# Re-ordering six places of a two-layer transformer kernel, and folding the last two batches' gates into copies of the down-projection weights

## The reference, cut to what matters

```python
# layer 0, single-head attention and MLP, conditioned by film scale and shift
h = film(rmsnorm(x, norm1_w), cond, film1_w, film1_b)
x = x + softmax(q(h) @ k(h).T * 128**-0.5) @ v(h) @ proj_w + proj_b
h = film(rmsnorm(x, norm2_w), cond, film2_w, film2_b)
x = x + gelu(h @ mlp_w1 + mlp_b1) @ mlp_w2 + mlp_b2
# layer 1, 16 heads of 8 channels, padding mask, six vectors per batch from silu(cond)
mod = silu(cond) @ ada_w.T + ada_b
shift_msa, scale_msa, gate_msa, shift_mlp, scale_mlp, gate_mlp = split(mod, 6)
h = layernorm(x) * (1 + scale_msa) + shift_msa
x = x + gate_msa * (attention(h, mask) @ proj_w.T + proj_b)
h = layernorm(x) * (1 + scale_mlp) + shift_mlp
x = x + gate_mlp * (gelu(h @ fc1_w.T + fc1_b) @ fc2_w.T + fc2_b)
```

## Time and profile before

| what | value |
|---|---|
| time of the runs, median (lowest to highest) | 193.1 us (192.03 to 194.94), 3 runs |
| the profiled execution: its own time | 191.69 us |
| its span, first to last instruction | 189.9 us |
| mean granted TensorE clock in the span | 0.990 |
| busy: TensorE, VectorE, ScalarE, GpSimd | 173.1, 121.1, 107.7, 98.7 us |

### The profile page before, as it was taken

One profiled execution on the slowest core, in us unless ns is written; L12 is line 12 of the kernel. 1 busy time (PEld: TensorE's weight loads), 2 busy tenths in 40 slices (PEclk: granted clock), 3 DMA queues, 4 the chain that ended last, 5 costly groups with the idle time before them and its releaser, 6 DMA issues.

```text
span 189.9 us, 5687 instructions
## 1 busy us (share of the span) xinstructions
PE 173.1 (91%) x2250; PEld 134.2 (71%) x2250; DVE 121.1 (64%) x357; ACT 107.7 (57%) x272; POOL 98.7 (52%) x166
## 2 busy tenths in 40 slices
PE   6876989999699999889999999996997999999993
PEld 6744877587276698677678777875886765678592
DVE  0693598978005069768756876699489665596233
ACT  2336957862683751577577756673774785723500
POOL 5599949899900805994004333675145086691000
PEclk9999999999999999999999999998899999999999
DMA  5999999412650300300110000100000000001103
GB/s 126 345 430 423 433 412 431 177 43 52 217 224 0 114 0 3 116 5 5 57 60 3 7 35 31 57 5 2 5 7 7 2 3 0 5 0 55 59 0 110
DMA packets 5190, 19.31 MB, mean 102 GB/s; under 512 B 556, under 2 KB 1148, under 8 KB 3836
## 3 DMA queue, kind: packets, MB, share of 16 engines
q1 hardware_dynamic: 4844, 18.27, 25.0%
q10 hardware_dynamic: 320, 0.68, 1.2%
HBM read 7.24 MB, written 1.09 MB: 44 GB/s over the span
## 4 chain that ended last, share of the span: by engine, by line
PE 44%; issue 20%; POOL 19%; DVE 9%; DMA 3%; ACT 3%; POOLq 0%; DVEq 0%; ACTq 0%
PE ps L337 8%; PE ps L328 7%; PE ps L315 6%; PE ps L307 6%; POOL xb L1196 3%; POOL gtmp L1194 3%; POOL xc L1189 3%; PE ps L265 3%; POOL rstd L1115 3%; PE ps L366 2%; DMA xs<-x 2%; POOL xs L1203 2%; POOL gated L1200 2%; ACT hT L661 2%; DVE bn L844 2%
## 5 line engine op out<-in xcount | busy, mean ns | idle before, releaser
L1002 DVE TENSOR_REDUCE nm<-ps 128x4 f32<-128x512 f32 x64 | 42.0, 683 | 18.3 <-PE ps L366 17.9
L739 ACT ACTIVATE shared<-ps 128x512 f32<-128x512 f32 x64 | 34.5, 596 | 22.0 <-PE ps L366 21.9
L366 PE MATMUL ps<-k_pad,q_pad 32*128 32x128 f32 x512 | 35.4, 284 | 5.0 <-DVE nm L1002 4.7
L366 PEld LDWEIGHTS ps<-k_pad,q_pad 32*128 32x128 f32 x512 | 30.1, 188 | 13.2 <-issue 6.5
L366 PE MATMUL ps<-q_pad,k_pad 32*128 32x128 f32 x512 | 35.5, 285 | 0.1
L366 PEld LDWEIGHTS ps<-q_pad,k_pad 32*128 32x128 f32 x512 | 29.7, 188 | 0.5 <-DMA q_pad<-nmT 0.5
L1115 POOL TENSOR_TENSOR rstd<-var_eps,half 128x4 f32<-128x4 f32 x16 | 16.4, 1023 | 24.5 <-DVE var_eps L858 17.0
L1200 POOL TENSOR_TENSOR gated<-attn,gate 128x128 f32<-128x128 f32 x16 | 7.3, 459 | 40.8 <-ACT attn L758 40.7
L432 PE MATMUL ps<-shared,vx 128*32 128x128 f32 x512 | 17.9, 282 | 0.5 <-ACT attn L758 0.3
L785 ACT ACTIVATE hid<-ps,W 128x512 f32<-128x512 f32 x16 | 10.9, 689 | 9.7 <-PE ps L328 9.7
L307 PE MATMUL ps<-hT,W 128*128 128x512 f32 x32 | 14.6, 598 | 1.7 <-ACT hT L661 1.7
(11 more groups left out here) (127 smaller groups left out, 321.9 us busy)
## 6 DMA issues: line engine op xcount, KB each, us to landing
q_pad<-hid SPq DMA_DIRECT2D x1, 4096.0 KB, 21.7
k_pad<-hid SPq DMA_DIRECT2D x1, 4096.0 KB, 30.6
gate<-gates SPq DMA_DIRECT2D x1, 2048.0 KB, 7.2
xs<-x SPq DMA_DIRECT2D x4, 256.0 KB, 6.4
gate<-mask SPq DMA_DIRECT2D x1, 1024.0 KB, 11.9
q_pad<-apT SPq DMA_DIRECT2D x4, 256.0 KB, 2.4
k_pad<-apT SPq DMA_DIRECT2D x4, 256.0 KB, 2.4
W<-weights SPq DMA_DIRECT2D x1, 768.0 KB, 9.9
```

Source lines behind the costliest of these rows:

```text
L366: return mm(bank(to)[:, t], held[some, t, b], moved[some, t, b], start=True, stop=True, skip_group_check=True)
L739: a(pT[b % 2][:, r], bank(of), ACT.Exp, scale=HD ** -0.5).then_inc(s["c_exp"], 1)
L1002: v.tensor_reduce(nm[b % 2][:, 4 * r:4 * r + 4], bank(of), AX.X, ALU.max, negate=True).then_inc(s["c_max"], 1)
```

## The change

Nothing of what is computed changes. In the order of the lists:

1. VectorE's silu(cond) goes from behind `a_residual(0)` to ahead of the first `hT` (its wait for `a_T`).
2. ScalarE does `a_kv(0)` ahead of `affine("a_", 1, ...)`.
3. `b_up(1)` and `b_gelus(1)` are cut in two halves, and the transposition and `affine` of group 2 stand between the halves.
4. V of the second group is made in two halves of two batches in bank 7, in `between(2)` and `between(3)` (`second_value`), and copied by ScalarE in two halves (`second_v`); `project_v(1)`, `front_v(1)` and the wait of `between(3)` for them are gone. `behind(3)` waits for the second half's copy.
5. `d_norm(0)` and `d_norm(1)` leave VectorE. GpSimd does them (`first_norm`), at its b = 11 and b = 15; its `d_bias(0)` moves from b = 11 to b = 12.
6. GpSimd makes, at b = 13 and 14, a copy of the `fc2` weights times the gate of batch 14 and of batch 15 (into `hc`, free by then). `d_last` uses them for the last two batches, each into a place of its own (banks 6 and 2), so that VectorE has one addition per batch in place of a multiplication and an addition for the pair. Each of the two is sent by itself: six transfers out instead of five.

```diff
-            for n, (b, size) in enumerate(((0, G), (G, G), (2 * G, G), (3 * G, 2), (3 * G + 2, 2))):
+            for n, (b, size) in enumerate(((0, G), (G, G), (2 * G, G), (3 * G, 2), (B - 2, 1), (B - 1, 1))):
...
+            def d_last(j, o_bank):
+                pe.wait_ge(s["d_w2"], j - 1)
+                for f in range(FC):
+                    ins = mm(bank(o_bank)[:, j], hid[1][:, f, j], hc[j % 2][:, f], start=(f == 0), stop=(f == FC - 1),
+                             skip_group_check=True)
+                ins.then_inc(s["d_M2"], 1)
...
+            def second_value(half):
+                if half:
+                    pe.wait_ge(s["c_vh"], 1)
+                for j in (2 * half, 2 * half + 1):
+                    mm(ps[:, 7, N * (j % 2):N * (j % 2) + N], hc[1][:, j], w("v1"), start=True, stop=True,
+                       skip_group_check=True)
...
-                if g % G < 3 and g // G + 1 < B // G:
+                if g % G < 3 and g != 2 and g // G + 1 < B // G:
                     pe.wait_ge(s[("c_q", "c_k", "c_v")[g % G]], g // G + 2)
...
                     pe.wait_ge(s["c_h"], b + LEAD)
+                    if b in (2, 3):
+                        second_value(b - 2)
                     turn_x(b + LEAD)
...
-                    pe.wait_ge(s["c_v"], (b - 3) // G + 1)
+                    pe.wait_ge(s["c_v"], max(2, (b - 3) // G + 1))
...
-                if g < B // G and b % G < 3:
+                if g < B // G and b % G < 3 and b != 2:
...
-            b_up(1)
+            b_up(1, range(2))
             m_norm("b_", 2, 4)
+            b_up(1, range(2, FC))
...
-            d_down(3, 6, range(2, 4))
+            d_last(2, 6)
+            d_last(3, 2)
...
+            a_kv(0)
             affine("a_", 1, 0, bank(0))
-            a_kv(0)
...
-            b_gelus(1)
+            b_gelus(1, range(2))
             affine("b_", 2, 1, bank(4))
+            b_gelus(1, range(2, FC))
...
+            def second_v(half):
+                v = ps[:, 7, 0:2 * N].rearrange("n (a k d) -> n a k d", k=2, d=HD)
+                slots = vx[1][:].rearrange("n b (a z) -> n (b a) z", z=64)[:, 16 * half:16 * half + 16]
+                for k in range(2):
+                    ins = a(slots[:, :, 48 * k:48 * k + HD], v[:, :, k], ACT.Copy)
+                ins.then_inc(s["c_v" if half else "c_vh"], 1)
...
                     front_h(b + LEAD)
+                if b in (2, 3):
+                    second_v(b - 2)
...
+            dve.wait_ge(s["silu_e"], 1)
+            v.tensor_scalar(cond_s[:], cond_e[:], 1.0, None, ALU.add).then_inc(s["silu_one"], 1)
+            dve.wait_ge(s["silu_one"], 1)
+            v.reciprocal(cond_r[:], cond_s[:]).then_inc(s["silu_one"], 1)
+            dve.wait_ge(s["silu_one"], 2)
+            v.tensor_tensor(silu[:], w("cond", B), cond_r[:], ALU.mult).then_inc(s["silu_ok"], 1)
             dve.wait_ge(s["a_T"], 1)
...
-                if b in (11, 14):
-                    d_norm((b - 11) // 3)
...
-            d_residual(3, 2, 2)
+            for j in (2, 3):
+                b = 3 * G + j
+                dve.wait_ge(s["d_M2"], 6 + j)
+                dve.wait_ge(s["d_xb"], 4)
+                v.tensor_tensor(xs[:, b], bank(6 if j == 2 else 2)[:, j], xb[:, b], ALU.add).then_inc(s["d_res"], 1)
...
+            def first_norm(g):
+                pool.wait_ge(s["d_pow"], g + 1)
+                for j in range(G):
+                    b = G * g + j
+                    ins = p.tensor_scalar(xn[g][:, j], xs[:, b], stat[:, b, 0:1], rstd[:, 3, b:b + 1], ALU.subtract, ALU.mult)
+                ins.then_inc(s["d_xn"], 1)
...
                 if b == 11:
+                    first_norm(0)
+                elif b == 12:
                     pool.wait_ge(s["c_xb"], b + 1)
                     d_bias(0)
+                elif b in (13, 14):
+                    pool.wait_ge(s["c_V"], G - 1)
+                    p.tensor_tensor(hc[(b + 1) % 2][:], w("fc2", F).rearrange("p (f c) -> p f c", f=FC),
+                                    gate[:, b + 1, 1, :].unsqueeze(1).broadcast_to((128, FC, C)), ALU.mult).then_inc(s["d_w2"], 1)
+                elif b == 15:
+                    first_norm(1)
```

More of the change, by code:

```diff
@@ L150, in build @@
             b_pow b_xn b_xb b_T b_h b_M1 b_gelu b_M2 b_res
-            c_pow c_xb c_gp c_xc c_Tx c_h c_Q c_K c_V c_q c_k c_v c_qs c_ks
+            c_pow c_xb c_gp c_xc c_Tx c_h c_Q c_K c_V c_q c_k c_v c_qs c_ks c_vh
             c_S c_max c_NT c_nm c_nms0 c_nms1 c_T c_exp c_PV c_oT c_T2 c_rden c_on c_T3 c_onT c_pr c_at c_ga c_res c_st
-            d_var d_pow d_xn d_xb d_T d_h d_M1 d_gelu d_M2 d_gm d_gp d_res""".split()
+            d_var d_pow d_xn d_xb d_T d_h d_M1 d_gelu d_M2 d_gm d_gp d_res d_w2""".split()
         s = {n: sem(n) for n in names}
@@ L299, in m_norm, with b_up @@
                 transposes(bank(t_bank), xn[g % 2], s[p + "T"])
-            def b_up(g):
-                for f in range(FC):
+            def b_up(g, fs=range(FC)):
+                for f in fs:
                     if f == 0:
@@ L695, in _, with b_gelus @@
                 a_exp(g)
-            def b_gelus(g):
-                for f in range(FC):
+            def b_gelus(g, fs=range(FC)):
+                for f in fs:
                     act.wait_ge(s["b_M1"], FC * g + f + 1)
@@ L725, in front_k @@
                 a(k_sb[:], bank(K_BANK[g]), ACT.Identity, bias=col("cols1", COL1["k_b"])).then_inc(s["c_k"], 1)
+            def second_v(half):
[4 more added lines that the diff above has]
+                ins.then_inc(s["c_v" if half else "c_vh"], 1)
             def front_v(g):
-                act.wait_ge(s["c_V"], g + 1)
+                act.wait_ge(s["c_V"], g + 1 if g < 2 else g)
                 v = ps[:, V_BANK[g], :].rearrange("n (a k d) -> n a k d", k=2, d=HD)
@@ L776, in step @@
                     front_k(b // G + 1)
-                elif b % G == 2 and b // G + 1 < B // G:
+                elif b % G == 2 and b > 2 and b // G + 1 < B // G:
                     front_v(b // G + 1)
@@ L946, in _ @@
                 dve.wait_ge(s["a_res"], G * (g + 1))
-                if g == 0:
-                    dve.wait_ge(s["silu_e"], 1)
-                    v.tensor_scalar(cond_s[:], cond_e[:], 1.0, None, ALU.add).then_inc(s["silu_one"], 1)
-                    dve.wait_ge(s["silu_one"], 1)
-                    v.reciprocal(cond_r[:], cond_s[:]).then_inc(s["silu_one"], 1)
-                    dve.wait_ge(s["silu_one"], 2)
-                    v.tensor_tensor(silu[:], w("cond", B), cond_r[:], ALU.mult).then_inc(s["silu_ok"], 1)
             statistics(1, 3)
@@ L970, in d_residual @@
                 rows = slice(j, j + n)
-                o = bank(6 if n < G and j else DOWN_BANK[g % 2])[:, rows]
+                o = bank(DOWN_BANK[g % 2])[:, rows]
                 v.tensor_tensor(gmul[g % 2][:, rows], o, gate[:, b:b + n, 1, :], ALU.mult).then_inc(s["d_gm"], 1)
```

2 lines of the change are left out of this document (1 added, 1 removed).

## The result

The kernel after takes 183.14 us (median of 4 runs, 182.28 to 184.02) against 193.1 (192.03 to 194.94): a ratio of 0.950, 95% interval 0.942 to 0.958, faster. The forecast was 184.4, range 182.8 to 187.0. The profiled execution takes 182.43 us, its span 180.7, at a granted clock of 1.000 (before 191.69, 189.9 and 0.990).

A forecast was written before the change was run, and what follows sets the result against it. TensorE, busy 173.1 of 189.9 us, was taken as the bound, so only its waits and slow clock could be won. 2.15 + 1.55 + 0.1 + 4.2 + 0.65 = 8.65 us off 193.1 gave 184.4 us, range 182.8 to 187.0.

The forecast's parts named there:

- The front (2.15): Stage a's first groups: moves 1 and 2 together win 2.15 us (0.75 less 0.05, plus 1.45), bounds 1.3 and 2.4.
- Move 3 (1.55): Stage b: `b_up(2)` starts 1.55 us earlier because `affine` of group 2 stands behind two gelus, not four; bounds 1.2 and 1.7.
- late next is `affine` again, by 0.3: Ahead of `b_up(2)` after move 3: `affine` of group 2 is still what comes late, by 0.3 us.
- Move 4 (0.1): Steps 2 and 3: V in two halves wins 0.1 us; bounds 0.3 lost and 0.4 won.
- All I book here is the nearer start: Move 4, ahead of `first_slot(3)`: only the slot's earlier start is counted, 0.1 us.
- no wait of TensorE on L1002 over 0.7 us: Sign of a right forecast: TensorE never waits over 0.7 us for VectorE's maximum (L1002).
- Move 5 (4.2): Steps 12 to 15: norms moved from VectorE to GpSimd win 4.2 us net; bounds 2.0 and 4.5.
- 0.4 new wait: Move 5's new cost: `between(13)` waits 0.4 us for ScalarE's `affine` of stage d.
- GpSimd's list (20.7 us of work in 20.8): From 125.5 us to `m_norm("d_", 1)`: GpSimd's work takes 20.7 us; with some waiting it is 0.3 us late.
- The rival that GpSimd binds: Steps 13 to 15: with durations 15% longer, GpSimd's work loses 2.2 us, giving 186.6 us; chance 14%.
- Move 6 (0.65): The end: one addition instead of two instructions wins 0.6 us, a smaller transfer about 0.05; bounds 0.4 and 0.8.
- The clock elsewhere (11%): Rival: the clock falls at another place, one stretch costing 1.7 us, giving 186.1 us; chance 11%.

The follow-up runs named there:

- kernel 4: The kernel before with move 5 alone; 188.24 us.
- kernel 1: The kernel after with move 5 undone: norms of groups 0 and 1 on VectorE again, GpSimd's `d_bias(0)` back at step 11; 189.47 us.
- 3: The kernel after with move 5 undone, plus 24 unread matmuls at the end of `between(12)`, ahead of the wait of step 12; 192.04 us.
- Kernel 2: The kernel after with the norms of groups 0 and 1 on VectorE again, but GpSimd's `d_bias(0)` kept at step 12; 186.49 us.
- 6: The kernel after with move 2 undone: `a_kv(0)` behind the `affine` of group 1 again; 186.08 us.
- the twelve kernels: The follow-up runs: four on what move 5 is made of, five undoing the other moves singly, three on what is left, one of these the kernel after unchanged.
- the one with late copies: The kernel after with GpSimd's two weight copies moved from steps 13 and 14 to the end of its program; 182.12 us.
- the two versions: The kernel after with late weight copies, 182.12 us; the same with group 0's norm ahead of `weighted(9)` and its `affine` on VectorE, 182.11 us.
- kernel 12: The kernel after with late weight copies, group 0's norm transposed ahead of `weighted(9)` and its `affine` on VectorE; 182.11 us.

## Why the prediction was right, and where it was not

- **The front (2.15).** 2.02 measured. The order of events was as worked out: the first scores 2.43 us earlier, second Q/K 1.54 (1.45 forecast). Undone from the kernel after, silu was worth 0.94 (0.75 forecast) and move 2 1.46; the two overlap by 0.4.
- **Move 3 (1.55).** 1.71, at the upper bound of 1.7. The term that was mis-sized is "late next is `affine` again, by 0.3": it ends 0.05 ahead of `b_up(2)`, which TensorE reaches without a wait.
- **Move 4 (0.1).** The step that failed: "All I book here is the nearer start". Undoing it costs 0.65 by the last matmul, over the bound of 0.4: about 0.2 at steps 2 and 3, 0.22 at a `weighted` five steps later and 0.27 near `m_norm(2)`, the last two behind a copy of ScalarE that starts 0.2 to 0.3 us earlier with the move. Why it does is open. The sign "no wait of TensorE on L1002 over 0.7 us" failed at this place too. The working had said that L360 lies beside a wait of `first_slot(3)`; with L360 gone from there, the wait shows, as 0.83 us. In the old order this slot has no wait, and the second slots of steps 2 and 3 wait 0.68 and 0.52; in the new one they wait 0.24 and nothing. The sum of the waits shrank from 1.20 to 1.07.
- **Move 5 (4.2).** 4.20 measured in the table and 4.33 alone (kernel 4). Its terms: 2.0 of wait (1.99), 1.7 of clock (1.54 in kernel 1 against the kernels after and 3), 0.4 new wait (0.49), 1.26 at step 15 (gone), GpSimd 0.3 late (0.24). Each is within 0.2, and that their misses cancel to 0.00 is luck. The prediction named the stretching of L867 by GpSimd but took it as a property of the place. Kernel 2 shows that it was the cause: without the collision the wait of step 12 is 0.43 us, and the clock stays full behind it. In kernel 1 this is worth 3.1 us. For the kernel before it is less, since from that slot to the transposed maxima of batch 12 it takes 5.76 us, against 4.64 at full clock with the new wait: 1.12 there, and with 1.56 of wait some 2.7 of the 4.2 us. That is an estimate from these traces; the kernel before with its bias alone moved was not run.
- **GpSimd's list (20.7 us of work in 20.8).** It held: four normalisings in 3.13 us, 0.78 each where 0.79 was forecast, the last ready 0.06 us before `m_norm(1)` starts. The rival that GpSimd binds, 14%, did not come up.
- **Move 6 (0.65).** 0.80 at the tail, about 0.7 net, since the weight copies cost about 0.1.
- **The clock elsewhere (11%).** It did not fall in the kernel after: no wait there is over 0.83 us. The argument against it, that the clock had stayed up behind 2.27 us, rested on one profile and does not hold: kernels 4 and 6 have a slow stretch behind this very wait. What the forecast did not see is that this rival sat in the kernel before.
- **The whole.** The traces give 9.43 us from Q/K where 8.65 were forecast. The 0.78 between are: front -0.13, move 3 0.16, move 4 0.60 (0.10 at its steps, 0.22 and 0.28 behind them), move 5 none, move 6 0.15. The median came out 1.26 us under the forecast; the other 0.5 hang on which starts and slow stretches a few runs catch, below. That the median of four lay inside the range is partly luck: six more runs of the same kernel have a median of 182.21, under its lower end of 182.8.

## What to carry to other kernels

When a small VectorE `tensor_scalar` out of SBUF has several durations in one trace, look for the GpSimd operation beside the long ones before moving work between engines: a shift by one step may give more than half of what a move gives, and every long GpSimd operation that is added must be placed against such instructions. A wait of 2 us on TensorE cost itself plus, in some executions, another 1.1 to 1.7 us of clock here, which one profile may or may not show; the mean granted clock of every run does. Judge a removed wait by how much earlier the last matmul ends, from a fixed landmark.

## What the runs showed of the hardware that I had not expected

**The same wait may or may not cost clock.** Waits of 2.27 us ahead of the first scores: no slow stretch in the kernel before, one in kernel 4 and one with move 2 undone. Waits of 2.38 us at step 15: a stretch in kernel 1, none in the profile of kernel 2, whose windows read 1.00 all along:

```profile
140.00:142.00 2.00, 0.43 (x12) 1.00 0.03 8
142.00:144.00 2.00, 2.00 (x68) 1.00 0.01 4
```

No wait of 1.74 us or less was followed by one in any trace. So the kernel before has two waits (2.27 and 1.99) that can each cost clock. Its 29 runs beside the twelve kernels spread from 190.6 to 195.2 us, while the kernel after's ten lie within 182.2 to 184.0. The mean granted clock of each run tells why. In each profile a slow stretch is 3.4 us at half clock, which takes 0.009 off the mean, and the 29 runs fall into three levels:

| mean granted clock | slow stretches | runs | us |
|---|---|---|---|
| 1.000 | none | 3 | 190.6 to 190.8 |
| 0.988 to 0.991 | as for one | 12 | 191.7 to 192.8 |
| 0.979 to 0.982 | as for two | 14 | 193.0 to 195.2 |

Most of the spread goes with the slow stretches, then; the last level has two clusters of its own, 193.0 to 193.5 and 194.6 to 195.2, as far apart as the starts of the next paragraph. From the first level to the second are 1.1 us at the lowest times. That is what either stretch costs this kernel by its traces, once the wait that it hides is taken off (1.11 in the front, 1.12 at step 12). So the change wins some 8.4 us against a run of the kernel before without a stretch (190.6 against 182.2), 9.5 against one with one (191.7), and 10.8 with two (193.0). One thing does not fit: one run each of kernels 2 and 3 reads 0.982, as for two stretches, though these kernels have one long wait.

**TensorE's start differs by 1.6 us between executions.** The matmuls ahead of the first real work (L245), in the kernel after and then in the one with late copies (ns, min/median/max):

```profile
L245 PE MATMUL ps<-ident x32: 274/388/580, 1.5 to 7.7; 128*128 128x128 f32 x32
```

```profile
L245 PE MATMUL ps<-ident x32: 421/421/582, 1.5 to 10.0; 128*128 128x128 f32 x32
```

In the second they never get faster, and Q/K of group 0 starts at 12.21 instead of 10.55, though the granted clock reads 1.00 in both. The 22 runs of the kernel after and of the two versions lie in two clusters, 181.95 to 182.43 and 183.63 to 184.02, with nothing between; the profile with the late start is one of 183.9. The Trainium skill, page "TensorE: Matmul & The Clock Gate", section "What's actually happening", says that the number of slow matmuls at a kernel's start varies from run to run. These two rows agree in that; as the granted clock reads 1.00 beside them, what slows them is not shown. Against differences of 0.2 us such clusters can't be averaged out in a few runs, and landmarks counted from a fixed event can show them.

**VectorE reading PSUM is not held.** In kernel 12 the four `affine` tiles on VectorE lie beside GpSimd's L1242 in the last timeline above and take 0.40 us each, as they do in the kernel after with GpSimd idle (0.40 each, at 164.26). The lock of experiments 1 and 2 was seen only for `tensor_scalar` from SBUF to SBUF.
